# Cross-attention with softmax maxima on VectorE: outputs in front of the row of maxima, quarters moved by one-element maxima

## What is computed

```python
x = x + _L0_xattn_ref(_layernorm(x), ctx_1024, Wq, Wk, Wv, Wp, bp)   # 16 heads of 32
x = x + _L0_attn_ref(_layernorm(x), ...)                             # self-attention
x = x + _L0_ffn_ref(_layernorm(x), W_fc, W_proj)                     # squared ReLU, five spike steps
```

```python
q = split(x @ Wq); k = split(y @ Wk); v = split(y @ Wv)
attn = softmax(einsum('bhid,bhjd->bhij', q, k) * SCALE, axis=-1)
out = einsum('bhij,bhjd->bhid', attn, v)
```

## Time and profile before

| what | number |
|---|---|
| median of three runs | 1887.72 us |
| the profiled execution's own time | 1886.98 us |
| its span, first to last instruction | 1885.0 us |
| mean granted TensorE clock | 0.986 of 2.4 GHz |
| PE matmul, busy | 1818.3 us (96%) |
| DVE busy | 1317.2 us (70%) |
| POOL busy | 888.0 us (47%) |
| ACT busy | 822.2 us (44%) |

### The profile page before, as it was taken

The page is one execution under the profiler, slowest core; times in us unless marked ns, Lnnn a source line. Parts: engine busy times, 40 slices in busy tenths (PEclk is TensorE's granted clock), DMA queues, the critical chain, the costliest instruction groups (busy, mean ns, idle before and its releaser), DMA issues. The chain is left out here.

```text
span 1885.0 us, 65763 instructions
## 1 busy us (share of the span) xinstructions
PE 1818.3 (96%) x28732; PEld 1573.4 (83%) x28732; DVE 1317.2 (70%) x1942; ACT 822.2 (44%) x982; POOL 888.0 (47%) x830
## 2 busy tenths in 40 slices
PE   8989999999999999999999999999999999999998
PEld 7868888879797979797988888888888877777887
DVE  5855959595959596868686867777676876575265
ACT  4624444454544454444444444444444433344332
POOL 0432727373737373737373636363645463444211
PEclk9989999999999999999999999999999999999999
DMA  7210202020202020202020202020201132033110
GB/s 258 93 52 2 81 3 80 3 80 3 80 3 80 3 80 3 80 3 80 3 80 3 80 3 80 3 80 5 78 10 72 38 109 90 24 91 99 48 56 23
DMA packets 43358, 101.19 MB, mean 54 GB/s; under 512 B 19120, under 2 KB 20656, under 8 KB 42960
## 3 DMA queue, kind: packets, MB, share of 16 engines
q1 hardware_dynamic: 43088, 96.88, 14.7%
HBM read 86.48 MB, written 8.29 MB: 50 GB/s over the span
## 5 line engine op out<-in xcount | busy, mean ns | idle before, releaser
L555 POOL TENSOR_TENSOR fold<-fold,prob 128x256 f32<-128x256 f32 (+1 forms) x704 | 718.4, 1020 | 71.3 <-ACT prob L606 17.0
L113 PE MATMUL ring<-y_parts,w_keep 128*128 128x402 f32 (+1 forms) x3072 | 613.4, 353 | 1.4 <-PEq L191 1.4
L113 PEld LDWEIGHTS ring<-y_parts,w_keep 128*128 128x128 f32 x3072 | 557.2, 190 | 17.0 <-issue 4.9
L113 PE MATMUL ring<-wv_s,y_parts 128*128 128x512 f32 x2304 | 550.5, 396 | 3.3 <-DVE v_sb L703 3.3
L113 PEld LDWEIGHTS ring<-wv_s,y_parts 128*128 128x128 f32 x2304 | 428.4, 188 | 109.6 <-DVE v_sb L703 13.1
L549 POOL TENSOR_TENSOR fold<-prob 128x256 f32<-128x256 f32 x64 | 57.1, 892 | 693.2 <-ACT prob L606 693.2
L575 ACT ACTIVATE k_sb<-ring 128x402 f32<-128x402 f32 (+1 forms) x256 | 129.5, 506 | 414.0 <-PE ring L113 414.0
L766 DVE TENSOR_TENSOR prob<-prob,peak_rows 128x1024 f32<-128x1024 f32 (+1 forms) x192 | 276.6, 1493 | 1.6
L600 ACT ACTIVATE prob<-s_ps 128x1536 f32<-128x1536 f32 (+1 forms) x128 | 200.0, 1562 | 127.5 <-PE s_ps L916 127.5
L731 DVE TENSOR_TENSOR fold<-fold,prob 128x512 f32<-128x512 f32 x192 | 166.6, 868 | 76.5 <-ACT prob L600 72.0
L606 ACT ACTIVATE prob<-prob 128x1024 f32<-128x1024 f32 (+1 forms) x192 | 205.4, 1120 | 0.0
(11 more groups left out here) (212 smaller groups left out, 1634.5 us busy)
## 6 DMA issues: line engine op xcount, KB each, us to landing
y_raw<-yT SPq DMA_DIRECT2D x48, 804.0 KB, 6.6
y_raw<-yT SPq DMA_DIRECT2D x16, 792.0 KB, 9.1
f_raw<-w_ffn SPq DMA_DIRECT2D x22, 512.0 KB, 3.5
v_sb<-y_left SPq DMA_DIRECT2D x1, 2304.0 KB, 11.2
v_sb<-v_left SPq DMA_DIRECT2D x16, 130.0 KB
p_x<-x SPq DMA_DIRECT2D x4, 512.0 KB, 6.6
q_scratch<-p_x SPq DMA_DIRECT2D x8, 256.0 KB, 2.1
q_sb<-q_scratch SPq DMA_DIRECT2D x16, 128.0 KB, 5.2
```

Source lines behind the costliest of these rows:

```text
L113: mm = pe.matmul(out, left(a, c), right(b, c), start=(c == 0 and n == 0), stop=(c == DC - 1 and n == 2))
L555: pool.tensor_tensor(acc[0:m], acc[0:m], prob[0:m, i, t, :], ALU.add).then_inc(sum_step, 1)
```

## The change

Five edits, all in `cross_attention`:

1. In `keys_phase`, `output(b-1, i)` for i = 1 and 2 stands in front of `row_of_peaks(b, i-1)`.
2. `value(b, 0)` stands in front of `row_of_peaks(b, 2)`. In batch 0 the whole loop over `left_value` and `left_low` stands in front of it too.
3. In `values_phase` the even value copies stand at other places between the softmax steps of block 3, and the first `low` stands behind `value(b, 8)`.
4. The six copies of 32 partitions x 8 in `row_of_peaks` are maxima over one element.
5. In the last weighing of batch 15, POOL adds seven tiles instead of thirteen (`LAST_SUM`), and PE adds the other six into the same PSUM sum: 24 more matmuls.

```diff
             def row_of_peaks(b, i):
...
                 for k, rows in others:
-                    dve.tensor_copy(quarters[first, k, :], quarters[rows, 0, :]).then_inc(row_step, 1)
+                    dve.tensor_reduce(quarters[first, k, :], quarters[rows, 0, :].unsqueeze(2), AX.X,
+                                      ALU.max).then_inc(row_step, 1)
...
                 for k, rows in others:
-                    dve.tensor_copy(peak[rows, :], peak[first, :]).then_inc(row_step, 1)
+                    dve.tensor_reduce(peak[rows, :], peak[first, :].unsqueeze(2), AX.X,
+                                      ALU.max).then_inc(row_step, 1)
...
                 for i in (1, 2):
+                    if past:
+                        output(b - 1, i)
                     row_of_peaks(b, i - 1)
                     subtract(b, i - 1)
                     largest(b, i, 0)
-                    if past:
-                        output(b - 1, i)
-                    elif i == 1:
+                    if not past and i == 1:
                         for j in range(LEFT_SLOTS):
                             left_low(j)
                     largest(b, i, 1)
                 if past:
                     output(b - 1, 3)
-                row_of_peaks(b, 2)
-                subtract(b, 2)
-                if not past:
+                else:
                     for j in range(LT):
                         if j % 2 == 0:
                             left_value(j)
                         if j + LEFT_SLOTS < LT:
                             left_low(j + LEFT_SLOTS)
+                value(b, 0)
+                row_of_peaks(b, 2)
+                subtract(b, 2)
 
             def values_phase(b, more):
-                value(b, 0)
+                value(b, 2)
                 largest(b, 3, 0)
-                value(b, 2)
                 largest(b, 3, 1)
+                value(b, 4)
                 row_of_peaks(b, 3)
-                value(b, 4)
+                value(b, 6)
                 subtract(b, 3)
+                value(b, 8)
                 if more:
                     low(b + 1, 0)
-                value(b, 6)
-                value(b, 8)
-                if more:
                     low(b + 1, 1)
...
-                pe.wait_ge(sum_step, SUMS * (block + 1))
+                pe.wait_ge(sum_step, SUMS * block + summed - 1)
                 for g in range(HB):
-                    mm = pe.matmul(at[g * DH:(g + 1) * DH, N:2 * N], ones[:, 0:DH], fold[:, i, g * N:(g + 1) * N],
-                                   start=True, stop=True)
+                    total = at[g * DH:(g + 1) * DH, N:2 * N]
+                    mm = pe.matmul(total, ones[:, 0:DH], fold[:, i, g * N:(g + 1) * N], start=True,
+                                   stop=(summed == JT))
+                    for t in range(summed, JT):
+                        m = jtile(t)
+                        mm = pe.matmul(total, ones[0:m, 0:DH], prob[0:m, i, t, g * N:(g + 1) * N], start=False,
+                                       stop=(t == JT - 1))
...
-            weigh(B - 1, 3, last_bank(3))
+            weigh(B - 1, 3, last_bank(3), LAST_SUM)
```

More of the change, by code:

```diff
@@ L49 @@
 ROW_N = 9
+LAST_SUM = 7
 PIECES = ((0, 4), (4, 8), (8, JT))
@@ L542, in _, with totals @@
         def _(pool):
-            def totals(b, i):
+            def totals(b, i, tiles=JT):
                 done, at = len(PIECES) * (NBLK * b + i), SUMS * (NBLK * b + i)
@@ L549, in totals @@
                 pool.tensor_tensor(acc, prob[:, i, 0, :], prob[:, i, 1, :], ALU.add).then_inc(sum_step, 1)
-                for t in range(2, JT):
+                for t in range(2, tiles):
                     if t in (PIECES[1][0], PIECES[2][0]):
@@ L555, in totals @@
                     pool.tensor_tensor(acc[0:m], acc[0:m], prob[0:m, i, t, :], ALU.add).then_inc(sum_step, 1)
-            with pool.Fori(0, B) as b:
+            with pool.Fori(0, B - 1) as b:
                 for i in range(NBLK):
                     totals(b, i)
+            for i in range(NBLK - 1):
+                totals(B - 1, i)
+            totals(B - 1, NBLK - 1, LAST_SUM)
             pool.wait_ge(x_in, 32)
@@ L922, in small_read, with weigh @@
                 reached(pe, o_out, NBLK * b + i + 1)
-            def weigh(b, i, at=small_ps):
+            def weigh(b, i, at=small_ps, summed=JT):
                 block = NBLK * b + i
```

## The result

The changed kernel takes 1816.36 us (median of 4 runs, 1815.28 to 1817.7), the kernel before 1887.56 (1885.27 to 1889.46): a ratio of 0.9624, 95% interval 0.9607 to 0.964. The forecast was 1824.7 us in a range of 1820 to 1842. The direction held, and the waits and slow stretches that the prediction named are gone.

What follows compares the result with a forecast made beforehand. PE was taken as the bound, matmuls under way 1818.3 of 1885.0 us. Terms 33.5 + 16.5 + 3.3 + 8.6 + 1.5 - 0.4 = 63.0 us off 1886.98 gave 1824.0, plus 0.7: 1824.7 us, range 1820 to 1842.

Steps and rivals of the forecast that it cites:

- waits for `o_sb`: Before the last weighing of 15 batches PE waits for outputs; all 33.5 us were to go.
- falls of the clock behind them: From that weighing to the first value tile, 11 batches lose 1.5 us each to a lower clock; 16.5 us to go.
- waits for `v_sb`: In the values phase, PE's 16 small waits for value copies were to go: 3.3 us.
- batch 0: Left-over tiles: the 8.6 us wait for a low part goes, plus 1.5 us at a lower clock.
- last weighing and the rest of cross-attention: Batch 15's last weighing: 24 more matmuls at 0.016 us put 0.4 us onto PE.
- Outputs in front: Keys phase: outputs 1 and 2 before the row of maxima remove 33.5 us of waits and 16.5 us of clock falls.
- rival B: Values phase up to tile 4: a new PE wait in each batch, 8 to 20 us, giving 1832 to 1844; 21%.
- Hidden, counts nothing: Row of maxima: one-element maxima at 0.2 us (bounds 0.16 to 0.42) are hidden beside PE and gain nothing.
- timetable of the values phase: DVE's value copies all come before due; tightest is tile 4, copied at 20.0 us, due 22.6, 2.6 to spare.
- Rivals A: Around the weighings: the clock falls anyway, 16.5 + 1.5 us are not gained, 1842.7 us; 6%.
- C: Batch 0: the low part waits for ACT's high part or a slot instead; up to 10.1 us stay, 1834.8; 6%.
- D: Row of maxima: one-element maxima above 1.3 us make DVE the bound and the kernel slower; 1909 at 1.4 us; 2%.

Runs made afterwards that it cites:

- the two runs with waits of 0.7 us: The kernel before with one-element maxima alone, 1833.93 us; the changed kernel with outputs 1 and 2 back behind the next block's first maxima, 1827.6 us.

## Why the prediction was wrong in size and right in kind

The start-to-start times of the two profiles divide the 71.4 us of span. The first term is the time from the start of PE's row before each last weighing to the weighing, the second from there to value tile 0, the third from value tile 0 to the end of the batch's last value tile, in all 16 batches:

| term | forecast | measured |
|---|---|---|
| waits for `o_sb` | 33.5 | 34.6 |
| falls of the clock behind them | 16.5 | 16.8 |
| waits for `v_sb` | 3.3 | 7.6 |
| batch 0 | 10.1 | 10.9 |
| last weighing and the rest of cross-attention | -0.4 | -0.1 |
| later stages | 0 | 1.1 |
| start, rest of the keys phases | 0 | 0.6 |

**The step that failed** is the term "PE's small waits for `v_sb` go: 3.3 us". It took the recorded idle time for the price. The run with tile 6 moved shows 0.48 us for a recorded 0.17, the run with the outputs alone 2.9 for 2.09 in three waits, the old values phase 0.74 for 0.46: some 0.3 us more for each wait before a value tile. A recorded wait runs from a modelled end of the matmul before, which lies behind the start that the next one would have had (28.07 us of matmuls start the next group 27.91 us after their own start). That is 0.16 us; another 0.10 is the first matmul behind the wait, which has 0.34 us to itself instead of 0.23. The same, smaller, is in the `o_sb` waits: 2.35 us from start to start for a recorded 2.28. The term measured 7.6 us, and its 4.3 us are half of what was missing: with 7.6 in the sum the forecast would have been 1820.4, just inside the range, which had left 4.7 us on the side of a larger gain. The `o_sb` term was 1.1 us short and batch 0 0.8. The 1.1 us of the later stages come from the fifth edit.

**Outputs in front.** Worked out as the whole 33.5 + 16.5 us of this edit. That attribution was wrong: alone the edit gives 18 us, since PE loses 34.8 us at the value tiles instead. The sum came out right by luck: the third and the fourth edit, which the prediction priced at 3.3 us and at nothing, were there to keep the gain, and one of them is needed. Of the values phase the prediction asked only whether the new order keeps up, not whether the old one would. With the old order, the copies and value tile 0 in front, PE's wait moves to tile 4 with its fall of the clock (1870.5). This is rival B's mechanism at the place that it named. In the changed kernel it does not occur, as the 2.2 us to spare at tile 4 show.

**One-element maxima.** "Hidden, counts nothing" holds beside the new order (1816.19 with copies) and fails without it: alone they give 53 us. They and the new places of the value copies are two cures for one wait: with both edits taken back 54 us are lost, with the maxima taken back none, with the places taken back 10. Their price was also outside the bounds: 148 to 155 ns, below the shortest copy of 158. The page "VectorE: DVE Perf Modes" of the Trainium skill, section "The perf-mode tier table", has a float32 copy run at twice the rate of `tensor_reduce`. At eight elements the trace shows nothing of it: the copy is the slower one. The page "SBUF — State Buffer" of the Trainium skill, section "Who interferes with whom", says that `tensor_reduce` never contends with GpSimd on this chip; the trace agrees, with 153 ns at most in 192 cases where copies took up to 705.

**Value copies, batch 0.** The timetable of the values phase held within 0.5 us for all value copies (only the subtraction of block 3 was 1.5 us sooner than worked out), and batch 0's wait went entirely: 10.9 us where 10.1 were forecast.

**Last weighing.** Forecast 0.4 us, measured 2.3 in its place. The 24 matmuls written are 48 in the trace (28780 against 28732 in all), and the 104 of a weighing are 52 written ones; so the 0.016 us was the price of half a matmul. Twice 0.4 is 0.8, which is what the run ordered by tile shows (1.15 against 0.39 us in the kernel before). The rest is order: the 0.016 us came from a stretch in which four column groups take turns, while the added ones of one group stand behind each other. It stayed unseen in the sum, because 1.1 us came back in the next stage and because in this profile PE's gap in batch 15's second weighing was 0.6 us shorter, and the 12 products behind it took 3.05 us at a clock of 1.00 instead of 4.61 at 0.62: chance, as the pause varies from run to run.

**Rivals A, C and D** are out. The clock fell in no keys or values phase of the changed kernel: weighing to tile 0 is 3.98 us in every batch. The page "TensorE: Matmul & The Clock Gate" of the Trainium skill, section "A second HAM failure mode: psum-queue depth-cycling", tells of repeated falls by short pauses alone. No such fall is seen here, nor in the two runs with waits of 0.7 us. Rival B did not occur, as said.

## What to carry to other kernels

Price a wait of the busiest engine by the time from start to start against an undisturbed copy of the same stretch, not by its recorded idle time, and add what the clock loses behind it. Before an edit is given the whole of a wait, ask what the engine reaches next when it comes early: here moving the outputs alone carried the wait over to the value tiles, and only shorter or reordered work in front of both deadlines removed it. A small float32 copy between SBUF tiles (here 32 x 8) beside a busy GpSimd can be replaced by a one-element maximum at no loss. It is worth something only where a wait of the busiest engine hangs on it: 53 us alone, nothing in the changed kernel.

## What the hardware showed that was not expected

- A maximum over one element (32 x 8) takes 148 to 155 ns beside GpSimd or not. A copy of the same shape takes 158 to 167 ns where no GpSimd instruction runs beside it, and up to 705 where one does: in the kernel before, all copies over 200 ns are of the second kind.
- The clock fell from 2.4 towards 1.2 GHz behind pauses of PE of 2.28 us (11 of 14 in the kernel before, 12 of 14 with tile 6 moved) and 2.16 us (12 of 15), and never behind those of 1.58, 1.35 or 0.7 us. The stretch behind took 1.5 us longer in the first case and 1.1 in the second. The length of the pause alone does not decide: in batch 15's second weighing the clock fell behind 2.04 us in the run with batch 0 alone (the 12 products behind took 4.62 us) and stayed up behind 2.68 us in the changed kernel with the old values phase (3.05 us).
- Recorded float32 matmuls of the form 128\*32 128x64 cost 0.014 us each when four column groups take turns (104 in 1.48 us), and 0.05 us when those of one group follow each other (56 in 2.70 us).
